# Values against column lanes: four lanes of 32 columns and sums from a tile of ones

## What is computed

```
q, k, v = heads of layernorm(x) @ w_qkv.T + b_qkv      # 16 heads of 32 features
scores = q @ k.T / sqrt(32), masked above the diagonal  # 2048 x 2048 for a head
attn = softmax(scores)
out = attn @ v                                          # 2048 x 32 for a head
x = x + out @ w_out.T + b_out
```

## Time and profile before

| | |
|---|---|
| median of 3 runs | 3015.97 us (3015.76 to 3017.94) |
| the profiled execution | 3017.42 us |
| its span, first to last instruction | 3015.3 us |
| TensorE busy | 2944.4 us, 98% |
| VectorE, ScalarE, GpSimd busy | 1811.3, 1057.7, 723.7 us |
| mean granted TensorE clock | 0.992 of full |

### The profile page before, as it was taken

One profiled execution on the slowest core, in us unless ns is written; L12 is line 12 of the kernel. 1 busy time (PEld: TensorE's weight loads), 2 busy tenths in 40 slices (PEclk: granted clock), 3 DMA queues, 4 the chain that ended last, 5 costly groups with the idle time before them and its releaser, 6 DMA issues. The chain is left out here.

```text
span 3015.3 us, 40553 instructions
## 1 busy us (share of the span) xinstructions
PE 2944.4 (98%) x14016; PEld 2227.7 (74%) x14016; DVE 1811.3 (60%) x3302; ACT 1057.7 (35%) x1809; POOL 723.7 (24%) x472
## 2 busy tenths in 40 slices
PE   6999999999999999999999999899999999999999
PEld 5788888888888878754454555578888888888887
DVE  5656655656565544666666665766565665565654
ACT  4322222222222232365565665343222222222222
POOL 3322222222222224300000002333222222222221
PEclk9999999999999999999999999999999999999999
DMA  3000000000000026722222232100000000000001
GB/s 98 28 22 29 22 27 21 21 28 26 22 28 21 1 57 135 221 52 49 60 48 53 59 82 63 51 22 28 22 26 23 28 21 28 21 21 28 25 10 56
DMA packets 120240, 126.85 MB, mean 42 GB/s; under 512 B 72728, under 2 KB 72984, under 8 KB 116820
## 3 DMA queue, kind: packets, MB, share of 16 engines
q1 hardware_dynamic: 120148, 125.71, 15.5%
HBM read 96.34 MB, written 29.34 MB: 42 GB/s over the span
## 5 line engine op out<-in xcount | busy, mean ns | idle before, releaser
L61 PE MATMUL psum<-ffn_x_high,ffn_w_high 128*128 128x512 f32 x2048 | 801.5, 391 | 16.9 <-POOL ffn_x_low L214 9.7
L62 PE MATMUL psum<-ffn_x_low,ffn_w_high 128*128 128x512 f32 x2048 | 798.2, 390 | 0.0
L63 PE MATMUL psum<-ffn_x_high,ffn_w_low 128*128 128x512 f32 x2048 | 797.9, 390 | 0.0
L591 POOL TENSOR_TENSOR ffn_inner<-ffn_gelu,ffn_inner 128x512 fp32r<-128x512 f32 x256 | 345.8, 1351 | 1169.1 <-ACT ffn_inner L529 1169.1
L436 DVE SCALAR_TENSOR_TENSOR ffn_gelu<-ffn_gelu,psum 128x512 f32<-128x512 f32 x256 | 175.9, 687 | 604.0 <-ACT ffn_gelu L522 604.0
L61 PEld LDWEIGHTS psum<-ffn_x_high,ffn_w_high 128*128 128x128 f32 x2048 | 385.0, 188 | 105.5 <-POOL ffn_x_low L214 10.2
L63 PEld LDWEIGHTS psum<-ffn_x_high,ffn_w_low 128*128 128x128 f32 x2048 | 385.2, 188 | 80.6
L62 PEld LDWEIGHTS psum<-ffn_x_low,ffn_w_high 128*128 128x128 f32 x2048 | 385.1, 188 | 78.6
L61 PE MATMUL psum<-ffn_inner,ffn_w_high 128*128 128x512 f32 x1024 | 398.6, 389 | 0.2
L62 PE MATMUL psum<-ffn_inner,ffn_w_high 128*128 128x512 f32 x1024 | 398.4, 389 | 0.0
L63 PE MATMUL psum<-ffn_inner,ffn_w_low 128*128 128x512 f32 x1024 | 398.4, 389 | 0.0
(11 more groups left out here) (112 smaller groups left out, 3048.2 us busy)
## 6 DMA issues: line engine op xcount, KB each, us to landing
ffn_words<-packed SPq DMA_DIRECT2D x96, 256.0 KB
ffn_word_scales<-scales SPq DMA_DIRECT2D x96, 256.0 KB
qk_parts<-parts SPq DMA_DIRECT2D x32, 512.0 KB, 4.2
queries<-qk_parts SPq DMA_DIRECT2D x48, 256.0 KB, 4.2
keys<-qk_parts SPq DMA_DIRECT2D x48, 256.0 KB, 6.1
x<-x_in SPq DMA_DIRECT2D x4, 1024.0 KB, 15.3
v_parts<-parts SPq DMA_DIRECT2D x16, 256.0 KB, 3.2
values<-v_parts SPq DMA_DIRECT2D x16, 256.0 KB, 7.2
```

The source lines that it names most:

```text
L61: pe.matmul(out, w_high, x_high, start=first, stop=False, skip_group_check=True)
L62: pe.matmul(out, w_high, x_low, start=False, stop=False, skip_group_check=True)
L63: return pe.matmul(out, w_low, x_high, start=False, stop=last, skip_group_check=True)
L591: pool.tensor_tensor(inner[:, tb % 2, m, 1, :], product[m], f32(inner[:, tb % 2, m, 0, :]), ALU.subtract)\
```

## The change

`out_bank` now has four lanes of 32 partitions. A tile of 128 keys meets a quarter of its block's queries in each: four values products of 128 columns (`value_lane`), and four more whose stationary operand is a tile of ones with 32 columns (`sum_lane`), which leave the sums in the bank's next 128 columns. On the diagonal the dead quarters are left out; except in the last head `diagonal_rounds` interleaves values and sums so that each lane gets five. Tiles now go block by block (3, 2, 1, 0), the diagonal ones together as the last batch of a block; `ORDER` goes, and `probs` has 12 places for 8. ScalarE copies 128x256 four times a head. SyncE stores four pieces of values and one of sums for each block, 20 transfers a head for 8. The head loops of VectorE and SyncE are written out; TensorE and ScalarE keep theirs. In the last head the projection takes block 3 ahead of block 2, the reciprocal is one of 128x128, and the product with it four of 32x128.

```diff
-def tiles_of_block(b):
-    diagonal = [4 * b + 3 - j for j in range(4)]
...
-LANES = [[(b, kt) for b in lane for kt in tiles_of_block(b)] for lane in ((3, 0), (2, 1))]
-TILES = [tile for pair in zip(*LANES) for tile in pair]
 BLOCKS = (3, 2, 1, 0)
+TILES = [(b, kt) for b in BLOCKS for kt in range(4 * b + 4)]
...
-RING = 2 * BATCH
+RING = 3 * BATCH
...
+def rows_of_values(q):
+    return quarter(QUARTERS - 1 - q)
+
+def rows_of_sums(q, last_head):
+    return rows_of_values(q) if last_head else quarter(q)
+
+def diagonal_rounds():
+    for r in range(BATCH + 1):
+        for lane in range(QUARTERS):
+            q = QUARTERS - 1 - lane
+            if r <= q:
+                yield "values", q, r
+            else:
+                yield "sums", lane, r - q - 1
...
-                last = pe.matmul(out_bank[row:row + columns, off:TB], values[i][:, kt, 0:columns],
-                                 probs[:, (SLOTS * s + t) % RING, 0:TB - off], start=(t in FIRST_OF_BLOCK),
-                                 stop=(t in LAST_OF_BLOCK), skip_group_check=True)
+            def value_lane(s, t, q):
+                b, kt = TILES[t]
+                col = (q - max(0, kt - 4 * b)) * P
+                return pe.matmul(out_bank[rows_of_values(q), 0:P], values[s % 3][:, kt, :],
+                                 probs[:, (SLOTS * s + t) % RING, col:col + P], start=(t in FIRST_OF_BLOCK),
+                                 stop=(t in OUT_DONE), skip_group_check=True)
+
+            def sum_lane(tile, q, j, last_head=False):
+                col = (q - j) * P
+                return pe.matmul(out_bank[rows_of_sums(q, last_head), P:2 * P], heads.ones[:],
+                                 tile[:, col:col + P], start=False, stop=False, skip_group_check=True)
+
+            def meet_batch(hp, s, i, last_head=False):
...
+                diagonal = t0 in DIAGONAL_TILES
+                if diagonal and not last_head:
+                    for kind, q, j in diagonal_rounds():
+                        last = value_lane(s, t0 + j, q) if kind == "values" else sum_lane(tiles[j], q, j)
+                else:
+                    for j in range(BATCH):
+                        for q in range(j if diagonal else 0, QUARTERS):
+                            last = value_lane(s, t0 + j, q)
+                    for j in range(BATCH):
+                        for q in range(j if diagonal else 0, QUARTERS):
+                            last = sum_lane(tiles[j], q, j if diagonal else 0, last_head)
...
-            with sp.Fori(0, HEADS // 3 - 1) as hp:
+            for hp in range(HEADS // 3 - 1):
...
-            with dve.Fori(0, HEADS // 3 - 1) as hp:
+            for hp in range(HEADS // 3 - 1):
...
+                act.activation(heads_out[:, e, :, :], out_bank[:, 0:2 * P], ACT.Copy).then_inc(out_free, 1)
...
+                    for q in range(QUARTERS):
+                        sp.dma_start(o_heads[bass.ds(h0 * HD + s * HD, HD), b * TB + q * P:b * TB + (q + 1) * P],
+                                     heads_out[rows_of_values(q), e, 0, :]).then_inc(out_stored[e], 16)
+                    sp.dma_start(sums[bass.ds(h0 + s, 1), cols(b, TB)].rearrange("o (q t) -> (o q) t", q=QUARTERS),
+                                 heads_out[0:P:HD, e, 1, :]).then_inc(out_stored[e], 16)
```

More of the change, by code:

```diff
@@ L651 @@
 FIRST_OF_BLOCK = [[tile[0] for tile in TILES].index(b) for b in BLOCKS]
-LAST_OF_BLOCK = [max(t for t in range(SLOTS) if TILES[t][0] == b) for b in BLOCKS]
 LAST_CHUNK = {b: max(m for m in range(SLOTS) if CHUNKS[m][0] == b) for b in BLOCKS}
[L654 to L659, removed]
+OUT_DONE = [max(t for t in range(SLOTS) if TILES[t][0] == b) for b in BLOCKS]
+NOUT = len(BLOCKS)
 SCORE_BANKS = 3
@@ L662 @@
 AHEAD = BATCH
-RING = 2 * BATCH
+RING = 3 * BATCH
 DIAGONAL_TILES = [t for t in range(SLOTS) if TILES[t][1] >= 4 * TILES[t][0]]
-ORDER = [t for j in range(0, SLOTS, BATCH)
-         for t in sorted(range(j, j + BATCH), key=lambda t: (t in DIAGONAL_TILES, t not in DIAGONAL_TILES and t % 2, t))]
-FIRST_SCORE = [u for u in range(SLOTS) if TILES[ORDER[u]][0] not in [TILES[t][0] for t in ORDER[:u]]]
+BATCHES = SLOTS // BATCH
 ROWS_AT = {3: 0, 19: 3, 31: 2, 39: 1}
@@ L722, in __init__ @@
         self.max_parts = sb("max_parts", [P, 2, 4, 2], F32R)
+        self.ones = sb("ones", [P, HD], F32)
         self.ident = sb("ident", [P, P], F32)
@@ L1154 @@
 LATE_K = KT - 1
-STEPS = [(b, k) for b in (2, 3, 1) for k in range(LATE_K)] + [(2, LATE_K), (3, LATE_K)]
+STEPS = [(b, k) for b in (3, 2, 1) for k in range(LATE_K)] + [(3, LATE_K), (2, LATE_K)]
 STEPS += [(0, k) for k in range(LATE_K)] + [(1, LATE_K), (0, LATE_K)]
@@ L1268, in attention @@
         out_free = sem("out_free")
-        out_stored = [sem(f"out_stored{e}") for e in range(len(OUTS))]
+        out_stored = [sem(f"out_stored{e}") for e in range(NOUT)]
         block = ctx.enter_context(nc.Block())
@@ L1274, in _, with store @@
         def _(sp):
[L1275 to L1284, removed]
+            def store(h0, s):
+                for e in range(NOUT):
+                    b = BLOCKS[e]
+                    sp.wait_ge(out_free, NOUT * h0 + (NOUT * s + e + 1 + 1))
+                    for q in range(QUARTERS):
[3 more added lines that the diff above has]
+                                 heads_out[0:P:HD, e, 1, :]).then_inc(out_stored[e], 16)
             def wait_for_stores(heads_stored):
-                for e in range(len(OUTS)):
-                    sp.wait_ge(out_stored[e], 32 * len(OUTS[e]) * (heads_stored + 1))
+                for e in range(NOUT):
+                    sp.wait_ge(out_stored[e], 80 * (heads_stored + 1))
             heads.load(sp, 2, 2)
@@ new lines, in sum_lane @@
+            def sum_lane(tile, q, j, last_head=False):
[3 more added lines that the diff above has]
+            def meet_batch(hp, s, i, last_head=False):
+                t0 = BATCH * i
+                tiles = [probs[:, (SLOTS * s + t0 + j) % RING, :] for j in range(BATCH)]
+                if t0 in FIRST_OF_BLOCK:
+                    pe.wait_ge(out_free, 3 * NOUT * hp + (NOUT * s + FIRST_OF_BLOCK.index(t0) + 1))
+                pe.wait_ge(probs_ready, 120 * hp + (SLOTS * s + t0 + BATCH))
+                diagonal = t0 in DIAGONAL_TILES
[9 more added lines that the diff above has]
+                            last = sum_lane(tiles[j], q, j if diagonal else 0, last_head)
+                if t0 + BATCH - 1 in OUT_DONE:
@@ L1379, in head @@
                     if t % BATCH == BATCH - 1:
-                        for v in range(t + 1 - BATCH, t + 1):
-                            with_values(hp, s, v)
+                        meet_batch(hp, s, t // BATCH)
             def project(n):
@@ L1412, in last_head @@
                             project(n)
-                        for v in range(t + 1 - BATCH, t + 1):
-                            with_values(hp, 0, v, columns=LANE)
+                        meet_batch(hp, 0, t // BATCH, last_head=True)
                 for n in BEHIND:
@@ L1566, in _ @@
         def _(pool):
-            pool.memset(start[:, 0:1], 0.0).then_inc(out_free, 3)
-            for e in range(len(OUTS)):
-                pool.memset(start[:, e + 1:e + 2], 0.0).then_inc(out_stored[e], 32 * len(OUTS[e]))
+            pool.memset(start[:, 0:1], 0.0).then_inc(out_free, 1)
+            for e in range(NOUT):
+                pool.memset(start[:, e + 1:e + 2], 0.0).then_inc(out_stored[e], 80)
             pool.wait_ge(o.wo_high_ready, 1)
```

88 lines of the change are left out of this document (35 added, 53 removed).

## The result

The changed kernel takes 3043.7 us (median, 3042.44 to 3045.62) beside 3016.95 us for the kernel before on the same chip: a ratio of 1.0088, 95% interval 1.0071 to 1.0106, so slower by 27 us. 3031 us had been forecast, with a range of 3012 to 3052 that took in two rivals; the forecast's own range, 3021 to 3041, was missed by 3 us. The profiled span grew from 3015.3 to 3040.7 us, by 25.4 us.

A forecast was written before the change was run, and what follows sets the result against it. TensorE, busy 98% of the span, was taken to bound the kernel. Terms -10.6 + 5 + 3 + 18 - 0.6 = +15 us gave 3017.4 + 15 - 1.4 = 3031 us, range 3012 to 3052 (own range 3021 to 3041).

The forecast's parts named there:

- rival D: Attention: the changed tile order costs 1 us a head by waits between ScalarE and three score banks, +12 us, 3043; chance 0.12.
- the 38.5 that was to show it wrong: Attention: heads longer than 38.5 us away from the jumps would refute the forecast of about 37.5 us.
- VectorE's three stops, -10.6: Attention: writing VectorE's loop out removes three stops at its jumps back, gain 10.6 us, bounds 7 and 10.6.
- Values, +5: Attention's values and sums in four lanes: 1.88 us a full batch, 1.23 a diagonal one, +5 us over 15 heads.
- rival C: Values batches: four lanes don't keep their rate for a whole batch, some +14 us a head, 3240; chance 0.05.
- Order of tiles, +3: Attention scores: diagonal tiles together wait for masks, 0.2 us a diagonal batch, +3 us in all, bounds -6 and +10.
- TensorE's loop body, +18: Attention: the longer body isn't held, four jumps back stop TensorE at 4.5 us each, 18 us, bounds 0 and 32.
- Rival A: Attention: TensorE's longer loop costs nothing, being held or its jump hidden, -3 us, 3013; chance 0.15.
- Rival B: Attention: fetching binds all along, each crossing stopping TensorE by 0.5 us, about 45 us, 3076; chance 0.08.
- the Trainium skill's rule: Head loops: TensorE holds 2048 instructions, other engines 512; a taken branch to code no longer held waits for a fetch.
- Last head, -0.6: Last head: batches +2.9 us, against shorter reciprocal chain and a wait removed; sum -0.6 us, bounds -4 and +3.
- Stores and loads, 0: SyncE: 20 transfers a head for 8, some 6 us issue a head, covered by 37 us of TensorE work.

The follow-up runs named there:

- experiment 2: The kernel before with VectorE's head loop alone written out: 3008.6 us, ratio 0.9966.
- experiment 3: The changed kernel with VectorE's head loop put back: 3043.7 us, ratio 1.0085 to the kernel before.
- Experiment 4: The changed kernel with the diagonal tiles of a batch scored narrowest first: 3023.8 us, ratio 1.0020 to the kernel before.
- experiment 1: The changed kernel with TensorE's head loop written out too: 3021.2 us, ratio 1.0011 to the kernel before.
- experiment 5: The changed kernel with TensorE's loop written out and diagonal tiles scored narrowest first: 3001.75 us, ratio 0.9943 to the kernel before.
- experiment 7: The kernel before, VectorE's loop written out, values products cut into calls of at most 256 columns in the same two lanes: 3013.8 us, ratio 0.9984.
- experiment 8: The kernel before with VectorE's and TensorE's loops both written out: 3009.6 us, ratio 0.9967.
- experiment 6: The kernel before, VectorE's loop written out, values products cut into calls of at most 128 columns in the same two lanes: 3096.8 us, ratio 1.0261.
- experiment 9: The kernel before, VectorE's loop written out, values products in pieces of 256 columns, ten full tiles a head in 128: 3062.4 us, ratio 1.0145.
- experiment 10: The kernel before, VectorE's loop written out, values products in pieces of 256 columns, sixteen full tiles a head in 128: 3074.2 us, ratio 1.0182.

## Why the prediction was right, point by point

The mechanism was right: four stops of TensorE at its jumps, of a size near the forecast's. The size of the whole was not: +15 forecast, +27 measured, and 3043.7 us lies in the range only because it took in rival D, which puts 3043. A regular head takes 38.07 us, half-way between the 37.5 forecast and the 38.5 that was to show it wrong. Two terms were too small, the order and the jumps.

- *VectorE's three stops, -10.6.* Right as a price (9.6 by itself, experiment 2), and right only beside the next point: with TensorE's loop as it is, the gain is no longer to be had (experiment 3). The forecast charged the whole of TensorE's stops and credited the whole of VectorE's, which comes to the same sum; that the overlap was left out did no harm is luck. The net price of TensorE's stops in place of VectorE's is 21.7 - 10.6, about 11 us.
- *Values, +5.* Right: 1.89 and 1.23 us, (6 x 1.89 + 4 x 1.23) - 15.9 = +0.36 us a head, +5.4. That rounds keep their pace over 64 records, which the trace of before could only show for 32, is shown; rival C falls.
- *Order of tiles, +3.* Right in kind, mis-sized: a head grew by 1.02 us, so 0.66 of it, +10 us over 15 heads, is left for what stands between the batches. That is the upper bound of the forecast and most of rival D. The step at fault took 0.2 us a batch from the earlier trace rows, a batch that opens with two full tiles. In one that opens with a diagonal tile of 512 the fourth score starts 0.39 to 0.51 us behind the product ahead of it, instead of 0.23. Experiment 4 confirms the place.
- *TensorE's loop body, +18.* Right in mechanism, number of stops and place; each cost 5.4 us for 4.5, +21.7. The idle time was 3.6 to 3.9 us where I took 3.1 from VectorE's stops, and the clock fell behind all four. The body is 3.1 times as long as before by the count of instructions (4132 for 1350), not 3.4. Rivals A and B are refuted by the stops themselves and by experiment 1.
- *The instruction counts.* The prediction says that the trace agrees with the Trainium skill's rule for VectorE's stops. In length it doesn't: VectorE's body has 458 instructions from branch to branch, fewer than the 512 that the prediction quotes, and wasn't held. ScalarE's, of 293, jumps at the same places and made no head long in experiments 1, 2, 5, 7 and 8.
- *Last head, -0.6.* From the 15th head's end to the last update of x it came to -1.2, inside the bounds of -4 and +3. *Stores and loads, 0*: no wait for them shows in the regular heads.

The sum was +15 and came to +25 in the profiled span: +7 from the order and +4 from the jumps, while the later start of attention and what lies behind the 15th head about cancel. Runs of both kernels differ by 27 us.

What stays open in part is why the idle time at a jump is 3.6 to 3.9 us in the changed kernel and 2.2 to 2.8 us in experiments 6, 9 and 10. About 0.6 us is work that still covers the jump: behind the trace's branch record TensorE is busy for another 0.72 us in the changed kernel and for 1.25 to 1.30 in the others. From the branch record to the next score it is 4.3 to 4.6 us there and 3.4 to 4.1 in the others, and that difference isn't explained. Length doesn't matter between 1974 and 2502 instructions (9.6 to 10.1 us of idle in all), but no body between 2502 and 4132 was run, and what stands ahead of the jump differs as well.

## What to carry to other kernels

When a change cuts work into more instructions, count the body of every hardware loop on that engine. The price of passing what is held is a stop at each jump, and it doesn't show in the cost of any operation; writing the loop out removes it, and fetching in a straight line cost at most some 1 us here. Savings on two engines that stop at one place don't add. And where a few banks rotate, let the batch open with the tile whose consumer is shortest.

## What was not expected of the hardware

- A TensorE loop body of 1734 instructions is held; one of 1974 is fetched anew at each jump, at 2.2 to 2.7 us of idle and 5.1 to 5.3 us with the clock.
- A TensorE that fetches 1.18 MB of code in 530 us of attention loses nothing by it in its regular heads, 38.07 us with the loop and without (experiment 1); the second head lost 1.1 us.
- VectorE's loop body of 458 instructions wasn't held: 2.8 to 3.2 us of idle at each jump.
- Products of 128 columns in two lanes are dearer than in four: 32 records in 2.39 us against 64 in 1.89 us. The stationary tiles differ too, 33 columns and 32, and that wasn't taken apart.
